# Merging GpSimd's elementwise instructions into one each, with a broadcast operand, in a fused attention, mixture and state-space kernel

## The reference

```
x = x + attn(layernorm(x))        # xn = rmsnorm(.) * norm_w; q, k, v; 16 heads, causal; returns xn + out @ Wo.T + bo
x = x + ffn(layernorm(x))         # base + shared + routed low-rank, 6 experts, top 2 of a softmax
x = x + ssm(layernorm(x))         # below
x = x + ffn(layernorm(x))

# ssm, per token t, 256 channels d, 16 states n:
xc    = silu(conv(x));  delta = softplus(xc @ Wd.T + bd);  B = xc @ Wb.T;  Cm = xc @ Wc.T
h     = exp(A * delta) * h + (delta * xc) * B
y     = sum over n of h[n] * Cm[n]
out   = (y * sigmoid(x @ Wg.T + bg)) @ Wo.T + bo
```

## Time and profile before

| | |
|---|---|
| median of 3 runs | 2216.88 us (2210.49 to 2220.23) |
| the profiled execution | 2220.23 us |
| its span | 2218.4 us |
| mean granted TensorE clock | 0.934 |
| VectorE busy | 1856.9 us (84%) |
| TensorE busy | 1819.8 us (82%) |
| ScalarE busy | 1289.4 us (58%) |
| GpSimd busy | 1171.1 us (53%) |

### The profile page before, as it was taken

One profiled execution on the slowest core, in us unless ns is written; L12 is line 12 of the kernel. 1 busy time (PEld: TensorE's weight loads), 2 busy tenths in 40 slices (PEclk: granted clock), 3 DMA queues, 4 the chain that ended last, 5 costly groups with the idle time before them and its releaser, 6 DMA issues.

```text
span 2218.4 us, 32220 instructions
## 1 busy us (share of the span) xinstructions
PE 1819.8 (82%) x10881; PEld 1082.1 (49%) x10912; DVE 1856.9 (84%) x2760; ACT 1289.4 (58%) x2260; POOL 1171.1 (53%) x994
## 2 busy tenths in 40 slices
PE   5789787888889798888888788888978888877775
PEld 2445444546355454645455454545545463535343
DVE  5444798989899897989899898989889897978784
ACT  2446566566756657575665656576565657463531
POOL 1110665656455564647465464756556474556682
PEclk8999899999989999999999899999999999888988
DMA  4312576667657665666767666666766666651110
GB/s 114 91 49 68 120 152 145 145 140 152 130 125 155 140 153 124 146 137 137 154 134 147 143 145 136 140 130 142 151 143 152 129 149 129 124 120 53 48 62 14
DMA packets 186054, 275.56 MB, mean 124 GB/s; under 512 B 33554, under 2 KB 125731, under 8 KB 185891
## 3 DMA queue, kind: packets, MB, share of 16 engines
q1 hardware_dynamic: 155650, 163.40, 28.9%
q0 software_dynamic: 30240, 110.11, 26.8%
HBM read 128.72 MB, written 34.08 MB: 73 GB/s over the span
## 4 chain that ended last, share of the span: by engine, by line
PE 31%; DVE 26%; DMA 14%; issue 12%; ACT 8%; POOL 5%; SPq 3%; DVEq 0%; POOLq 0%; ACTq 0%
DVE hc L1090 9%; PE bank L313 7%; DMA y<-hc 5%; DVE hc L1097 4%; POOL inp L1262 4%; PE bank L322 4%; DMA sk<-qk_parts 3%; DMA qk_parts<-parts 3%; PE bank L503 3%; PE bank L357 2%; PE bank L486 2%; PE bank L405 2%; PE bank L380 2%; DVE mall L975 2%; SPq L698 2%
## 5 line engine op out<-in xcount | busy, mean ns | idle before, releaser
L1262 POOL TENSOR_TENSOR inp<-u,b_all 128x512 f32<-128x512 f32 x512 | 731.8, 1469 | 333.7 <-DVE hc L1090 222.0
L1090 DVE TENSOR_TENSOR_SCAN hc<-dec,inp 128x1024 f32<-128x1024 f32 x256 | 672.4, 2627 | 20.7 <-ACT dec L864 19.3
L767 ACT ACTIVATE pt<-bank 128x512 f32<-128x512 f32 x640 | 375.2, 598 | 253.0 <-PE bank L382 251.1
L357 PE MATMUL bank<-sk,sq 96*128 96x512 bf16 (+3 forms) x1024 | 281.7, 314 | 131.9 <-DVE mall L973 52.3
L1269 POOL DMA_DIRECT2D y<-hc x210 | 186.0, 886 | 353.9 <-DMA y<-hc 162.5
L864 ACT ACTIVATE dec<-dt,a_neg 128x511 f32<-128x511 f32 x512 | 338.5, 719 | 39.4 <-DVE hc L1090 39.4
L1097 DVE TENSOR_TENSOR hc<-hc,bank 128x1024 f32<-128x1024 f32 x242 | 293.3, 1212 | 25.5 <-PE bank L542 24.9
L380 PE MATMUL bank<-sq,sk 98*128 98x512 bf16 (+3 forms) x1024 | 276.4, 308 | 15.3 <-DMA sq<-hlt 10.3
L973 DVE TENSOR_REDUCE mall<-bank 128x1 f32<-128x512 f32 x256 | 172.5, 674 | 138.6 <-PE bank L359 138.4
L357 PEld LDWEIGHTS bank<-sk,sq 96*128 96x128 bf16 x1024 | 102.9, 100 | 279.4 <-DVE mall L973 80.0
L313 PE MATMUL bank<-xt_q,wqk 128*128 128x512 f32 x256 | 153.6, 731 | 73.8 <-ACT bcs L844 67.9
(11 more groups left out here) (152 smaller groups left out, 3271.6 us busy)
## 6 DMA issues: line engine op xcount, KB each, us to landing
y<-hc POOLq DMA_DIRECT2D x210, 512.0 KB, 5.5
b_all<-b_kept SPq DMA_DIRECT2D x256, 256.0 KB, 4.3
qk_parts<-parts SPq DMA_DIRECT2D x96, 256.0 KB, 3.1
sq<-qk_parts SPq DMA_DIRECT2D x384, 64.0 KB, 3.4
sk<-qk_parts SPq DMA_DIRECT2D x384, 64.0 KB, 3.6
X<-in_x SPq DMA_DIRECT2D x16, 512.0 KB, 7.9
out<-X SPq DMA_DIRECT2D x16, 512.0 KB, 3.0
sq<-hlt SPq DMA_DIRECT2D x256, 2.0 KB
```

The source lines that it names most:

```text
L357: mm(dst[:, o:o + n], sq[0:KS, slot, h, qb * P:(qb + 1) * P], sk[0:KS, slot, h, 0:n], start=True, stop=False)
L767: A(pt[:, n % PT, :], score_bank[unit % 2][:, :], ACT.Exp).then_inc(exp_done.sem, 1)
L1090: V.tensor_tensor_scan(h, d, v, 0.0, ALU.mult, ALU.add).then_inc(scan_done.sem, 1)
L1262: last = G.tensor_tensor(inp[:, n % 2, c, :], u[:, c, :], b_all[:, k % 3, :], ALU.mult)
```

## The change

Three helpers of GpSimd issue one instruction where they issued two or four. In `weigh` the row of weights is read with a stride of 0 over the four blocks of tokens; in `inputs` the row of B is read with a stride of 0 over the two halves of the channels. Waits, semaphores and their counts stay as they are, and so does what is computed.

```
 def weigh(a):
     for c in range(C):
         pool.wait_ge(side["xn", c].full, side["xn", c].at("xn", a, c))
-    for tb in range(TB):
-        last = G.tensor_tensor(tok_q[:, tb, :], tok_q[:, tb, :], w_row[:, :], ALU.mult)
-    last.then_inc(weighed.sem, 1)
+    G.tensor_tensor(tok_q[:, :, :], tok_q[:, :, :], w_row[:, None, :].to_broadcast([P, TB, D]),
+                    ALU.mult).then_inc(weighed.sem, 1)

 def residual(a):
     pool.wait_ge(weighed.sem, weighed.at(a))
-    for j in range(2):
-        rows = X[:, a % XS, 2 * j:2 * j + 2, :]
-        last = G.tensor_tensor(rows, rows, tok_q[:, 2 * j:2 * j + 2, :], ALU.add)
-    last.then_inc(res_done.sem, 1)
+    G.tensor_tensor(X[:, a % XS, :, :], X[:, a % XS, :, :], tok_q[:, :, :], ALU.add).then_inc(res_done.sem, 1)

 def inputs(s, n):
...
-    for c in range(C):
-        last = G.tensor_tensor(inp[:, n % 2, c, :], u[:, c, :], b_all[:, k % 3, :], ALU.mult)
-    last.then_inc(inp_ready.sem, 1)
+    G.tensor_tensor(inp[:, n % 2, :, :], u[:, :, :],
+                    b_all[:, k % 3:k % 3 + 1, :].to_broadcast([P, C, T]),
+                    ALU.mult).then_inc(inp_ready.sem, 1)
```

## The result

The changed kernel takes 2248.57 us in the median of 4 runs (2244.77 to 2254.51), the kernel before 2215.48 in the median of its now 4 runs. The ratio is 1.015 with a 95% interval of 1.012 to 1.018: slower by 1.5%, as forecast (2251 us). The profiled execution took 2246.16 us, 25.9 more than that of before; the medians lie 33.1 apart. The profiled execution of before (2220.23) is the longest of its four, and that of the changed kernel lies 2.4 us under its median, so the traces hold less than the medians differ by. What follows explains the 25.9, since that is what the two traces hold.

What follows compares the result with a forecast made beforehand. VectorE (busy 84%) was taken as what matters, GpSimd as hardly on the path. Four terms gave +3.3 us a batch, +40 over 12 batches, +30 counted; with tail +4, +34: 2251 us (65%), range 2208 to 2272.

Steps and rivals of the forecast that it cites:

- Price of a merged instruction, 2.36 us: GpSimd's merged 128x1024 product was to last 2.36 us, where two 128x512 take 2.49.
- The rival at 1.94: Cheaper instruction: a merged product takes 1.94 us, each block is 0.42 shorter, 2213 us in all; chance 12%.
- Held for the whole length: Two-input operations of VectorE and GpSimd exclude each other; a merged one keeps VectorE out until 2.23 us after its start.
- Router +3.0 us a batch: L1034 to L1058 beside weigh, residual and next inputs: three long blocks delay L1058's end by 3.0 us.
- three quarters of everything: Of +40 us over 12 batches, +30 was counted; the last quarter was to be taken up where VectorE idles later.
- Gating of y +1.1: L1103 can no longer slip in after a pair's first half and waits 1.1 us longer a batch.
- Scan at n = 8 and the pair behind the DMA issue, -0.3: One scan waits 1.1 us longer; a later scan's 1.38 us wait behind a DMA issue goes; together -0.3 a batch.
- the faster rival: GpSimd issues its DMA earlier and blocks by pairs right behind an issue go, 4.1 us a batch: 2205 us; chance 14%.
- Second half waits -0.5: Scans that come in a pair's second half wait 0.14 us less each, -0.5 us a batch.
- Tail +0.2 a step: Some 20 steps after 1960 us, scan and inputs alternating: 4.65 us a step instead of 4.44, +4 us in all.
- VectorE busy +30 to 50, a larger scan mean: Sign of being right: VectorE busy 30 to 50 us more at the same instruction count, with a larger mean scan time.
- The upper end, 2272 us: Dearest form of the forecast: 2.50 us a merged instruction, some 0.3 more a block; all 40 on the path gives 2261.

Runs made afterwards that it cites:

- the one-part and moved kernels: Against the kernel before: inputs alone merged 0.993; weigh and residual alone merged 1.014; weigh and residual later in GpSimd's queue, full change 0.991, kernel before 1.007.
- The kernel with a pair at n = 3: Full change with weigh and residual moved later in GpSimd's queue and the inputs of n = 3 left in a pair: 2184.37 us, 0.986 of the kernel before.
- the kernel with all merged: Full change with weigh and residual moved later in GpSimd's queue (-39 instead of -57), inputs merged at every step: 2197.14 us, 0.991 of the kernel before.
- the two kernels with L1236 at 264: Full change, weigh and residual moved, second L1236 at 264 instead of 268: all inputs merged 0.980; inputs of n = 3 in a pair 0.975 (2162.14 us).
- the same move: Weigh and residual put at -39 instead of -57 in GpSimd's queue: full change 1.015 to 0.991, kernel before to 1.007.

## Why the prediction was right, and what it had wrong

- *Price of a merged instruction, 2.36 us:* 2.356 measured. The rival at 1.94 is out.
- *Held for the whole length:* shown, by L1034, L1039 and L1043, and by the one-part and moved kernels.
- *Router +3.0 us a batch:* from the scan's start to L1058's end it is 10.94 us and was 7.89: +3.05. It arrives whole at the scan of n = 6 (+3.0), in every batch of the second to the thirteenth. I had allowed three quarters of everything; of this item nothing was hidden, since the chain there was VectorE's.
- *A term that the sum lacks, the wait for TensorE:* the prediction took the router's loss as 3.0 us and no more. Behind it TensorE's granted clock falls and VectorE waits for TensorE at L1019: its idle time in the step of n = 9 is 1.24 us a batch, and was 0.35. That is +0.9, which hides two thirds of what the scan of n = 9 gives back.
- *Gating of y +1.1:* L1103 is 1.08 longer, but only +0.8 shows at the next scan and +0.3 at the one after it. The kernel with a pair at n = 3 agrees in its trace (its last scan starts 3.7 us earlier than in the kernel with all merged, 0.2 a batch from the second to the thirteenth and the rest at the ends). Its ratio says 0.5%, 12 us. The profiled execution of the kernel with all merged is the shortest of its six (2189.68, median 2197.14), which accounts for 7.5 us of this. And between the two kernels with L1236 at 264 the pair at n = 3 is worth 1.05 us a batch in the traces: what the gating's 1.1 is worth depends on what lies behind it.
- *Scan at n = 8 and the pair behind the DMA issue, -0.3:* the mis-sized term. The loss was as forecast (+1.1), the give-back 2.5 instead of 1.4, and would have been 3.4 without the wait for TensorE: the block at n = 10 or 11 went too (the 2.6 us at 946.78; in other batches L985 or L987). I had kept that in the faster rival and argued against it with the DMA issue's wait for a landing (4.47 us). In the changed kernel the issue still waits for a landing (1.89 us), but the scan that stood, now at 955.04, starts 0.83 us ahead of it (955.87). So a part of the faster rival came true beside the forecast. That rival had the scan of n = 11 stand in every batch, where two of 12 do; and its 1.38 + 2.62 are 4.0 us and not 4.1.
- *Second half waits -0.5:* the scan at 898.41 waited 0.27 and now waits 0.15 (2.43 at 902.18). The scans of n = 1, 5 and 13 are each 0.14 shorter in the mean of the 12 batches, -0.4 a batch: right.
- *Tail +0.2 a step:* 4.65 against 4.44. Its sum was +2.3, not +4: four steps, the last ones, grew by 0.2 each, and of the others some lost 1 us at a time and some gave back.
- The total was +1.9 a batch, not 3.3 or three quarters of it (2.5); 25 us where I had 34. The factor of three quarters stood for losses taken up where VectorE idles. That shows only at the gating, behind which VectorE's idle time at n = 2 fell by 0.4; what else made the total smaller was the larger give-back. The median's 33 lies closer to the forecast than the mechanism's own account does, and some of that is luck.
- *VectorE busy +30 to 50, a larger scan mean:* +25, and a smaller one (2604 ns, was 2627). A falling scan mean was among the prediction's own signs of being wrong. What scans lost at n = 8 (+1.08 us on the mean of that step) and in the tail they won at n = 9 (-1.37) and n = 11 (-0.45).
- *The upper end, 2272 us:* the "0.3 more a block" beside it doesn't follow from 2.50 - 2.36 = 0.14 us. The 11 us from 2261 to 2272 are about what 0.14 gives for five blocks a batch and the tail.

## What to carry to other kernels

Fewer and longer instructions on GpSimd are not free for VectorE: where both work on two SBUF operands, count what VectorE has beside each place, and merge where it has nothing, split where a small operation must get in, and move what needn't be there. Look for tiny operations with a large maximum in the single-line view; busy time hides them. Where VectorE stands, see what TensorE's granted clock does right behind. And time a move before keeping it: the same move gave 2.3% in one kernel and cost 0.7% in the other. Before merging anything that is not on the path, ask what it holds shut while it runs.

## What the runs showed that was not expected

- An operation of VectorE that started 0.1 to 0.7 us after GpSimd's start of a DMA issue waited not for the issue alone (0.88 us) but for what stood right behind it: L987 3.35 us for a pair, the scan 3.79 us for L1236. It isn't so for every operation: scans that started 0.37 and 0.47 us after an issue in the changed kernel, with L1229 (128x4) starting 0.67 us after the issue, took 2.28 to 2.29 us, and L1229 waited for them (2.8 and 2.9 us); in the kernel before, L985 or L987 took 0.17 us when it started within 0.03 us of the issue. That the long waits go with an issue and an instruction right behind it is shown by the times; why, the traces don't tell.
- An operation of VectorE need not read two tensors to be held. L985 reads one (a `tensor_scalar`) and stood up to 3386 ns; L1013, of the same kind, took 1.97 us or more in 13 batches of the kernel before with weigh and residual moved. The reductions with one input (L973, L1041) were not held. Which other operations are, these runs don't sort out.
- A pair right behind an issue takes 2.79 us instead of 2.50 and didn't let the scan in between its halves (3.67 at 929.93). The Trainium skill (Perfetto Trace Analysis, section on the GPSIMD engine's instruction) says that each of the engine's eight processors keeps an execution queue of its own, with no synchronization between them but what an instruction itself brings. Some of them lagging behind the issue might look like this; no run here shows it.
- The span minus VectorE's busy time was 362 us in both kernels and between 344 and 383 in all 13, while the span ran from 2160 to 2247.
